# Layer 0's pairwise gate: two neighbouring tiles in one VectorE instruction of 4,096 columns, the row terms stored by tile, the makers in a pattern of eight

## The reference, cut to what matters

```python
def step(hsum, inp):
    h_t, t = inp
    hsum = hsum + h_t
    hm = hsum / (t + 1.0)
    Pu = hm @ Wu.T
    Pv = hm @ Wv.T
    pre = jax.nn.relu(Pu[:, :, None, :] + Pv[:, None, :, :] + b1)
    S = jax.nn.sigmoid(jnp.einsum('bvud,d->bvu', pre, w2) + b2)
    a_t = jnp.einsum('bvu,bud->bvd', Aa[None, :, :] * S, h_t)
    m_t = h_t * jnp.einsum('vu,bud->bvd', Am, h_t)
    z_t = bet[0] * h_t + bet[1] * (a_t @ W_add.T) + bet[2] * (m_t @ W_mod.T)
    return (hsum, z_t)
```

## Time and profile before

| what | us |
|---|---|
| median of 3 runs | 25,409.81 |
| the runs | 25,401.43 to 25,497.12 |
| span of the profiled execution, first to last instruction | 25,493.9 |
| layer 0's tiles on VectorE, first start to last end, in that span | 152.8 to 5,912.8 |

### The profile page before, as it was taken

One profiled execution on the slowest core, in us unless ns is written; L12 is line 12 of the kernel. 1 busy time (PEld: TensorE's weight loads), 2 busy tenths in 40 slices (PEclk: granted clock), 3 DMA queues, 4 the chain that ended last, 5 costly groups with the idle time before them and its releaser, 6 DMA issues. The chain is left out here.

```text
span 25493.9 us, 384771 instructions
## 1 busy us (share of the span) xinstructions
PE 20717.4 (81%) x134800; PEld 8220.3 (32%) x134800; DVE 15361.5 (60%) x15737; ACT 14120.3 (55%) x22694; POOL 9395.5 (37%) x7816
## 2 busy tenths in 40 slices
PE   6888888884368888888859999997348888888899
PEld 2333333331122222222225444454013333333344
DVE  8999999994167777777835555555133333333111
ACT  6999998994257777777636665665222222222111
POOL 6777777782057777777720010001000000000000
PEclk9999999997678888888877776777679999999999
DMA  1000000006810000000031111112960011001111
GB/s 63 12 12 12 12 12 12 12 12 127 155 47 17 17 18 16 18 18 16 16 79 26 28 33 28 26 28 62 193 149 22 22 29 26 22 22 27 39 38 44
DMA packets 1295345, 995.42 MB, mean 39 GB/s; under 512 B 742248, under 2 KB 1151440, under 8 KB 1258968
## 3 DMA queue, kind: packets, MB, share of 16 engines
q1 hardware_dynamic: 1193416, 849.62, 15.9%
q0 software_dynamic: 26624, 100.67, 1.4%
q10 hardware_dynamic: 74448, 33.14, 0.5%
HBM read 771.60 MB, written 211.63 MB: 39 GB/s over the span
## 5 line engine op out<-in xcount | busy, mean ns | idle before, releaser
L270 DVE TENSOR_TENSOR l_mx<-l_p_v,l_puN 128x2048 f32<-128x2048 f32 x2560 | 5635.2, 2281 | 137.0 <-PE l_p_s L485 124.5
L485 PE MATMUL l_p_s<-l_mx,l_w2z 128*32 128x512 f32 x32768 | 3815.3, 610 | 579.5 <-ACT l_mx L397 307.9
L290 POOL TENSOR_TENSOR l_mx<-l_pv,l_puP 128x2048 f32<-128x2048 f32 x1024 | 3715.5, 3644 | 312.8 <-PE l_p_s L485 307.0
L1196 POOL TENSOR_TENSOR l1m_hc<-l1m_hs,l1m_cs 128x512 f32<-128x512 f32 x2304 | 2923.9, 1269 | 8.5 <-DVE l1m_hs L1148 8.1
L2072 PE MATMUL l3a_p<-l3a_xn,l3a_w 128*128 128x512 f32 (+1 forms) x6144 | 2682.9, 600 | 266.2 <-ACT l3a_xn L1963 266.2
L1148 DVE TENSOR_TENSOR_SCAN l1m_hs<-l1m_da,l1m_carry,l1m_pu 128x512 f32<-128x512 f32 x2304 | 2824.1, 1268 | 106.1 <-ACT l1m_da L1066 2.2
L2178 POOL DMA_DIRECT2D l3b_xt<-x_after x64 | 33.9, 529 | 7634.9 <-DVE l3b_most L2307 5811.9
L1790 ACT ACTIVATE l1d_ab<-l1d_pt 128x1024 f32<-128x1024 f32 x2304 | 2316.1, 1023 | 671.3 <-PE l1d_pt L1552 327.7
L416 ACT ACTIVATE l_mx<-l_pv,l_puP 128x128 f32<-128x128 f32 x8192 | 2446.7, 393 | 0.8
L1668 DVE TENSOR_SCALAR l1d_hat<-l1d_ab 128x1024 f32<-128x1024 f32 x2304 | 1917.0, 833 | 474.0 <-ACT l1d_ab L1790 363.6
L1587 PE MATMUL l1d_po<-l1d_hat,l1d_ring 128*32 128x128 f32 x36864 | 1893.2, 335 | 325.2 <-DVE l1d_hat L1668 214.1
(11 more groups left out here) (300 smaller groups left out, 27330.4 us busy)
## 6 DMA issues: line engine op xcount, KB each, us to landing
n_xt<-x_after SPq DMA_DIRECT2D x48, 2048.0 KB
l3a_xb<-x_after SPq DMA_DIRECT2D x352, 256.0 KB, 4.0
l1o_img<-x_after SPq DMA_DIRECT2D x32, 2032.0 KB, 17.5
l_img<-x_after SPq DMA_DIRECT2D x32, 2032.0 KB, 16.9
l1m_sq<-seq SPq DMA_DIRECT2D x256, 144.0 KB
n_xt<-in_x_dram SPq DMA_DIRECT2D x16, 2048.0 KB
l_xs<-in_x_dram SPq DMA_DIRECT2D x128, 256.0 KB, 2.8
x_after<-l_ot SPq DMA_DIRECT2D x128, 256.0 KB, 2.4
```

What stands on the lines that cost most here:

```text
L270: v.tensor_tensor(mx[:, r % QB, :, :, :], columns.unsqueeze(1).broadcast_to([P, 4, G, P]), rows.broadcast_to([P, 4, G, P]), ALU.max).then_ ...
L290: g.tensor_tensor(mx[:, r % QB, :, :, :], pv[:, u, :, :].unsqueeze(1).broadcast_to([P, 4, G, P]), rows.broadcast_to([P, 4, G, P]), ALU.add ...
L485: ins = pe.matmul(p_s[R * q:R * (q + 1), 512 * u:512 * (u + 1)], w2z[:, 31 - r:63 - r], mx[:, r % QB, q, :, :].rearrange("p t v -> p (t v) ...
L1196: g.tensor_tensor(hc[:, (3 * u + p) % 6, part, :], hs[:, p % 3, part, :], cs[:, u, :], ALU.mult).then_inc(hc_done, 1)
```

## The change

`MAKERS` has period "agvvgvvv" where it had "agvvvgvv": the counts stay, the second GpSimd tile of each eight moves from place 5 to place 4, so tiles 5, 13, 21 and 29 become VectorE's, and 4, 12, 20 and 28 GpSimd's. Two neighbouring "v" of which the first is even (2 and 3, 6 and 7 of each eight) are made by one VectorE instruction, which waits until both places are free and signals both tiles at its end; tile 5 stays single. So that both tiles' rows can be read in one pattern, ScalarE writes `puN` with the four rows of a tile side by side, the tiles following each other; its writes then step by four elements. The corrections use `puP` and w2 where they used `puN` and -w2.

```diff
-MAKERS = "agvvvgvvagvvvgvvagvvvgvvagvvvgvv"
+MAKERS = "agvvgvvvagvvgvvvagvvgvvvagvvgvvv"
 def layer0_maker(r):
     return MAKERS[r]
+
+
+def opens_pair(r):
+
+    return r % 2 == 0 and r + 1 < len(MAKERS) and MAKERS[r:r + 2] == "vv"
+
+
+def closes_pair(r):
+    return r > 0 and opens_pair(r - 1)
...
-                    if maker[r] == "v":
-
-                        v.wait_ge(dot_done, i * R + (r + 1))
-                        rows = puN[:, u, :, :].rearrange("p t (g r) -> p g t r", r=R)[:, :, :, r:r + 1]
+                    if maker[r] == "v" and not closes_pair(r):
+                        n = 2 if opens_pair(r) else 1
+
+                        v.wait_ge(dot_done, i * R + (r + n))
+                        rows = puN[:, u, :, :].rearrange("p t rq -> p rq t")[:, 4 * r:4 * (r + n), :].unsqueeze(3)
                         columns = p_v[:, 512 * u:512 * (u + 1)].rearrange("p (t c) -> p t c", t=G)
-                        v.tensor_tensor(mx[:, r % QB, :, :, :], columns.unsqueeze(1).broadcast_to([P, 4, G, P]),
-                                        rows.broadcast_to([P, 4, G, P]), ALU.max).then_inc(max_by_v, 1)
+                        v.tensor_tensor(mx[:, r % QB:r % QB + n].rearrange("p n q t c -> p (n q) t c"), columns.unsqueeze(1).broadcast_to([P, 4 * n, G, P]),
+                                        rows.broadcast_to([P, 4 * n, G, P]), ALU.max).then_inc(max_by_v, n)
...
-                act.activation(puN[:, un, :, :], p_t[:, :], ACT.Identity, scale=-1.0, bias=nb1[:, 0:1]).then_inc(pu_ready, 1)
+                act.activation(puN[:, un, :, :].rearrange("p t (r q) -> p t q r", q=4), p_t[:, :].rearrange("p (t q r) -> p t q r", t=G, r=R), ACT.Identity, scale=-1.0, bias=nb1[:, 0:1]).then_inc(pu_ready, 1)
...
-                    ins = pe.matmul(p_m[:, t:t + 1], puN[:, un, t, :], nw2[:, :], start=True, stop=True)
+                    ins = pe.matmul(p_m[:, t:t + 1], puP[:, un, t, :], w2c[:, :], start=True, stop=True)
```

More of the change, by code:

```diff
@@ L134, in layer0 @@
     maker = [layer0_maker(r) for r in range(R)]
-    made_by = {e: maker.count(e) for e in "vag"}
+    made_by = {e: maker.count(e) for e in "vagh"}
     xg = x.rearrange("b (q t) c d -> (b q) c t d", t=G)
@@ L156, in layer0 @@
         w2c = m.sb("w2c", [P, 1])
-        nw2 = m.sb("nw2", [P, 1])
         b2c = m.sb("b2c", [P, 1])
@@ L243, in _ @@
             v.tensor_copy(w2z[:, 31:32], w2c[:, :])
-            v.tensor_scalar(nw2[:, :], w2c[:, :], -1.0, None, ALU.mult)
             v.tensor_scalar(nb1[:, :], b1c[:, :], -1.0, None, ALU.mult)
```

## The result

The changed kernel took **25,721.3 us** (median of 4 runs, 25,681.3 to 25,865.6), the kernel before, in the same four rounds, 25,405.6 (25,344.0 to 25,497.1). The ratio is **1.014, 95% interval 1.0091 to 1.019**: slower, by 316 us in the medians, where 355 was forecast. The profiled execution has a span of 25,719.6 us.

What follows compares the result with a forecast made beforehand. The prediction took a loop through ScalarE, TensorE, GpSimd and SyncE to bound layer 0, not VectorE. Pairs 0 + moved tile 203 + clock 147 + row terms 5 = 355 us on 25,409.8: 25,765 us, range 25,560 to 25,890.

Steps and rivals of the forecast that it cites:

- What bounds the kernel: Layer 0: a loop through ScalarE, TensorE, GpSimd and SyncE sets the time, not VectorE, though busy 977.5 of 1,000 us.
- rival 2: Layer 0: VectorE sets the time after all; 25,335 us, or 25,198 with its stops gone too; chance 0.06.
- just two waits: ScalarE's waits in a group: 1.12 us for the mix and 2.35 for the load, both inside the loop.
- The pairs, priced at nothing: VectorE's gate tiles: 1,024 fewer starts save it 75 us, which only add to its stops; time cost 0.
- The margin of 0.3 us: Even group, pair of tiles 6 and 7: signalled some 0.3 us before TensorE would have to wait for it.
- The moved tile, 203 us: GpSimd's extra 3.60 us tile ahead of weigh_sums delays the copy of aT by 3.19 us in two groups: 203 us.
- The clock, 147 us: TensorE, idle longer before the sums, then runs at half speed: 1.4 us a group, 178 less 31, net 147 us.
- The row terms, 5 us: ScalarE's puN write stepping by four elements, priced from a two-step row at 0.04 us a group: 5 us, ends 0 and 88.
- The range's upper end: Whole time if slow stretches cost 1.7 us and the puN write doubles: given as 25,896, say 25,890 us.
- Rival 1: TensorE's clock holds because its idle time is broken up, while the wait still comes: 25,618 us; chance 0.22.
- Rival 3: The wait is absorbed by an earlier GpSimd tile 12 or ScalarE's idle times: 25,410 us; chance 0.07.
- Rival 4: VectorE's 4,096-column instruction takes longer than two of 2,048; 0.2 us more would cost some 100 us; chance 0.03.

Runs made afterwards that it cites:

- e9: Kernel before with SyncE's two small table loads issued a group earlier, nothing else of the change: layer 0 5,629 us, ratio 0.9912.
- e7: Changed kernel with the old MAKERS pattern and puN written in a row, leaving only the pairs: layer 0 5,780 us, one run.
- e1: Changed kernel with the old MAKERS pattern, pairs and stepped puN write kept: layer 0 5,843 us, ratio 1.0032.
- e5: Kernel before with only the stepped puN write and its reads and corrections, single tiles: layer 0 5,806 us, one run.
- e4: Changed kernel with two unused 512-column matmuls a group added on TensorE ahead of the weighted sums: layer 0 6,024 us, ratio 1.0131.
- e3: Changed kernel with weigh_sums put ahead of GpSimd's tile 12 instead of behind it: layer 0 5,830 us, ratio 1.004.
- e6: e3 with puN written in a row and the bank read in steps of 32 elements: layer 0 5,786 us, ratio 1.0021.
- e2: Kernel before with only the new MAKERS pattern, single tiles and plain puN write: layer 0 6,157 us, ratio 1.0169.

## Why the prediction came out

**What bounds the kernel.** Right, and now by experiment, not by reading alone: with the loop shortened (e9) layer 0 went down to VectorE's own time, 131 us under before, so before that VectorE was not the bound. That also settles rival 2. That ScalarE has "just two waits" was not the whole of it: before, it also waited 0.39 us a group ahead of the relus and 0.17 for the projections, and both come back below.

**The pairs, priced at nothing.** Right (e7: 5,780 for 5,760 and 5,773). They save a little less than reckoned: VectorE's busy time fell by 48 us in the changed kernel, where 75 was forecast. And the mark that would have spoken against the prediction, waits for pairs of over 0.5 us a group, was met: 100.2 us in 117 groups, 0.86. The margin of 0.3 us at tile 6 of the even group was too small a one, since the stepped write puts the start of VectorE's next group back by 0.52; without it the wait is 35.4 us (e7) for 134.0 (e1). What made it harmless is the part that did hold: behind it stands the wait for `asg`, which hides it. Where no such wait stands behind it, it may have a price: e1 (pairs and stepped write) is 37 us longer than e5 (the write alone), one execution of each. In the timeline of the changed kernel's even groups the two waits add up to nearly the same, 0.48 + 2.56 above, and in another one 2.37 + 0.74:

```profile
3145.19 1.93 PE L493 MATMUL l_p_s<-l_mx,l_w2z 128*32 128x512 f32 x16 [2.37 <-DVE l_mx L278]
3147.86 1.16 PE L476 MATMUL l_p_a<-l_asg,l_h 128*128 128x128 f32 x8 [0.74 <-POOL l_asg L320]
```

Where the wait was divided like this, in 40 groups of 117, the sums took 1.16 us, at full speed.

**The moved tile, 203 us.** Right in mechanism, and in size: e4 against e3 is 6,024 - 5,830 = 194, and in both the sums run at full speed (283 and 288 ns a record, 337 in the changed kernel). By waits it is 1.62 us x 127 = 206, though a part of that is the slowed sums.

**The clock, 147 us.** Right in kind, too high in size: after against e4 is 127, and since in e4 nothing is slowed here in any group, this stands beside the 178 that the prediction had before it took off 31 for slow mixes. The price of a group was right, the number of groups was not. The prediction took 1.4 us in every group. From the start of the sums to the end of the mix the changed kernel takes 6.53 us on average in the 77 groups with one long wait and 5.03 in the other 40: 1.50 us, but in two groups of three, which is 125 us in 127 groups. The place was only half seen, too. The slow stretch falls on the sums and on tile 8 more often than on the mix (54, 67 and 43 groups); the prediction counted tile 8 as free, but the mix stands behind it, so a tile 8 of 1.90 us is late for the mix, which shows as the wait at `zs`.

**The row terms, 5 us: the mis-sized term.** The write took 1,209 ns for 690, 66 us by itself, near the upper end of 88; the step of two elements was the nearest row, and nothing like it. The prediction set beside it the rule of the Trainium skill (SBUF — State Buffer, on cachelines), by which the sum would lie toward the upper end. That rule was the better guide: e5 and e6 together show that it is the write's step that costs. Even so it cost the changed kernel nothing: the write alone is worth 33 to 46 us (e5), but e2, which hasn't got it, is as long as the changed kernel. The waits of ScalarE show where it went. Per group, from after's and e2's rows, the changed kernel has 0.52 more for the write, and less at `aT` (1.62 for 1.85), at `zs` (2.17 for 2.27) and before GpSimd's relu (0.02 for 0.26), with 0.09 more at `pv`: +0.52 - 0.23 - 0.10 - 0.24 + 0.09 = +0.04. In e2, without pairs to divide the wait, 80 groups of 117 have something slowed behind it, for 68. That the smaller waits at `aT` and `zs` come from TensorE's wait being divided by the pairs, and the clock kept by it in some groups, fits the rows above, but no run separates it.

**The sum.** 355 against 391 in layer 0 and 316 in the medians. That the medians came out 75 us below layer 0's loss lies with layers 1 to 3, whose length wanders, and that 355 lies between the two is luck. Along one path the runs divide the 391 by terms: 26 from before to e6, 44 to e3 (the write), 194 to e4 (the moved tile), 127 to the changed kernel (the clock), where the prediction had 0, 5, 203 and 147. So the first two were 65 too low and the last two 29 too high. The terms do not simply add, though: along the other path e2 has 397 of it, and pairs and write on top of that nothing. Along that path the step that fell short is the moved tile with its clock, 350 for the 397 of e2. By waits a group of e2 is longer by 1.85 at `aT`, 0.90 at `zs`, 0.44 at `pv`, less 0.13 before the relu, in all 3.06, 389 us in 127. The prediction had the first two, at 1.60 and 1.16 together 2.76. The third, ScalarE's wait for the projections, it had not; in the two executions of before it is 20.5 and 47.9 us, so some 25 to 55 us of it are the change's. What makes it longer was not tried, and whether it lengthens a group is open: e6 has the same wait, 75.4 us in 124 groups, and is 26 us longer than before. The range's upper end has a slip of 10 us: its terms add up to 25,886, not 25,896; nothing hangs on it.

**Rival 1**, the clock holds, forecast 25,618: e4 is that rival made by hand, and the changed kernel lies 127 us above it in layer 0. **Rival 3**, absorbed: ruled out by the wait at `aT`. **Rival 4**: a pair is shorter than two tiles.

## What to carry to other kernels

An engine with 97% busy time need not be the bound; here nobody waited for it. Read the waits in both directions before saving time on it, and shorten the loop that does set the time first. When a pattern of work is rearranged for one engine, go through every step that stands at a fixed place in the other engines' lists, and see what now stands ahead of it: here one tile of 3.6 us passed one short step. And look at the granted clock behind a new wait on TensorE: here one wait of some 2.5 us cost 1.5 us more behind it on average, while two waits of 3.0 to 3.1 us together, with two tiles between them, cost no clock at all.

## What was not expected of the hardware

- ScalarE's copy of 512 columns to memory in steps of four elements (16 bytes) took 1,209 ns, in a row 690; reading the bank in steps of 32 elements and writing in a row took 690 as well. So in this kernel the steps of the transposing copy belong on the bank's side.
- Two extra matmuls a group made layer 0 shorter by 127 us, with the granted clock at 0.96 instead of 0.93.
- An idle time of TensorE of 2.34 to 2.69 us was followed by slowed matmuls in 68 groups of 77; divided by two tiles, though longer in all, in none of 40.
- Layers 1 to 3, with unchanged code, took from 19,568 to 19,789 us in the twelve profiled executions. The longer runs have the lower granted clock over the whole span (of the kernel before, 25,258 us at 0.880 and 25,508 at 0.867). What decides it is open; it is as large as most of the effects studied here, which is why a stage's own length was the measure.
